# Dividing self-attention probabilities by their sums before they are turned, instead of dividing the attention output

## The reference

```python
qkv = jnp.roll(h @ w_qkv + b_qkv, -SHIFT, axis=1).reshape(B, nw, WIN, 3, H, D)
q, k, v = (qkv[:, :, :, 0], qkv[:, :, :, 1], qkv[:, :, :, 2])
scores = jnp.einsum('bnqhd,bnkhd->bnhqk', q, k) / jnp.sqrt(jnp.float32(D))
attn = jax.nn.softmax(scores, axis=-1)
o = jnp.einsum('bnhqk,bnkhd->bnqhd', attn, v).reshape(B, L, C)
x = x + (jnp.roll(o, SHIFT, axis=1) @ w_so + b_so) * g_msa
```

## Time and profile before

| what | value |
|---|---|
| median of 3 timed runs | 1449.89 us (1449.7 to 1450.29) |
| the profiled execution | 1451.27 us, with a span of 1449.4 us |
| mean granted TensorE clock | 0.989 of full speed |
| TensorE busy | 1414.2 us, 98% |
| VectorE busy | 1015.7 us, 70% |
| ScalarE busy | 838.8 us, 58% |
| GpSimd busy | 427.6 us, 30% |

### The profile page before, as it was taken

One profiled execution on the slowest core, in us unless ns is written; L12 is line 12 of the kernel. 1 busy time (PEld: TensorE's weight loads), 2 busy tenths in 40 slices (PEclk: granted clock), 3 DMA queues, 4 the chain that ended last, 5 costly groups with the idle time before them and its releaser, 6 DMA issues.

```text
span 1449.4 us, 30030 instructions
## 1 busy us (share of the span) xinstructions
PE 1414.2 (98%) x9753; PEld 1197.5 (83%) x9753; DVE 1015.7 (70%) x4628; ACT 838.8 (58%) x2555; POOL 427.6 (30%) x613
## 2 busy tenths in 40 slices
PE   7989999999999999999999999999999999999997
PEld 5778788888888888888888788888888888887886
DVE  3486859587695868769595786959586785958532
ACT  3474475757566385756647476664757457574433
POOL 1314132233324232331335132233334213232302
PEclk9889999999999999999999999999999999999999
DMA  7520000010000000010010000000010000000000
GB/s 244 190 78 2 1 4 23 2 33 9 19 30 16 1 2 25 1 34 5 22 32 1 15 2 15 11 24 11 9 48 1 16 1 8 2 1 9 1 4 12
DMA packets 27340, 34.98 MB, mean 24 GB/s; under 512 B 3324, under 2 KB 22448, under 8 KB 26929
## 3 DMA queue, kind: packets, MB, share of 16 engines
q1 hardware_dynamic: 27185, 33.07, 7.1%
HBM read 28.83 MB, written 4.22 MB: 23 GB/s over the span
## 4 chain that ended last, share of the span: by engine, by line
PE 88%; DVE 7%; ACT 2%; issue 1%; SPq 0%; POOL 0%; DMA 0%; DVEq 0%; ACTq 0%; POOLq 0%
PE bank L955 13%; PE bank L910 13%; PE bank L979 11%; PE bank L962 7%; PE bank L919 6%; PE bank L783 6%; PE bank L769 5%; PE bank L842 4%; PE bank L830 4%; PE bank L894 4%; PE bank L822 2%; DVE knocked L2172 2%; PE bank L754 2%; PE bank L740 2%; PE bank L804 1%
## 5 line engine op out<-in xcount | busy, mean ns | idle before, releaser
L910 PE MATMUL bank<-hB,Wm 128*128 128x256 f32 x1024 | 243.8, 384 | 2.2 <-ACT hB L1341 2.2
L910 PEld LDWEIGHTS bank<-hB,Wm 128*128 128x128 f32 x1024 | 191.6, 191 | 33.8 <-issue 7.0
L955 PE MATMUL bank<-nxT,W1nx 128*128 128x256 f32 x896 | 212.8, 384 | 0.0
L1380 ACT ACTIVATE prob<-bank,rmax 128x128 f32<-128x128 f32 x512 | 180.0, 434 | 27.6 <-DVE rmax L2120 27.6
L1731 POOL TENSOR_TENSOR scores<-scores,M 128x308 f32<-128x308 f32 x128 | 94.3, 737 | 320.0 <-DVE knocked L2172 317.5
L1387 ACT ACTIVATE probT<-bank 128x512 f32<-128x512 f32 (+1 forms) x256 | 139.7, 615 | 82.9 <-PE bank L894 76.7
L979 PE MATMUL bank<-W2p,gT 128*128 128x256 f32 x768 | 183.2, 381 | 3.0 <-DVE acc L2251 1.9
L955 PEld LDWEIGHTS bank<-nxT,W1nx 128*128 128x128 f32 x896 | 166.6, 191 | 23.4 <-issue 2.8
L979 PEld LDWEIGHTS bank<-W2p,gT 128*128 128x128 f32 x768 | 141.2, 190 | 23.8 <-issue 2.8
L1419 ACT ACTIVATE tbs<-bank,b1half 128x256 f32<-128x256 f32 x128 | 60.6, 473 | 144.9 <-PE bank L910 103.2
L1435 ACT ACTIVATE tbs<-bank,betaH 128x256 f32<-128x256 f32 x224 | 95.3, 487 | 83.1 <-PE bank L962 83.1
(11 more groups left out here) (230 smaller groups left out, 2710.1 us busy)
## 6 DMA issues: line engine op xcount, KB each, us to landing
Wm_g<-in_L_xcond_w_m_dram SPq DMA_DIRECT2D x4, 1024.0 KB, 5.5
W1ev<-in_L_xcond_e_w_dram SPq DMA_DIRECT2D x6, 512.0 KB, 7.4
x<-in_x_dram SPq DMA_DIRECT2D x16, 128.0 KB, 2.7
x<-in_x_dram SPq DMA_DIRECT2D x32, 64.0 KB, 2.3
Wm<-in_L_xcond_w_m_dram SPq DMA_DIRECT2D x1, 2048.0 KB, 9.0
out_dram<-acc SPq DMA_DIRECT2D x16, 128.0 KB, 1.7
out_dram<-acc SPq DMA_DIRECT2D x32, 64.0 KB, 2.0
batch_rows<-row_store SPq DMA_DIRECT2D x4, 384.0 KB, 3.7
```

The lines of the kernel that those rows point to most:

```text
L910: m = pe.matmul(bank_of(name)[:, half * UT:(half + 1) * UT], Wm1[:, k, c:c + P], hB[:, k, :], start=(k == 0), stop=(k == CB - 1))
L955: pe.matmul(bank_of(name)[:, n * UT:(n + 1) * UT], W1nx[:, k, c0 + n * P:c0 + (n + 1) * P], nxT[:, k, :], start=(n == 0 and k == 0), stop= ...
L1380: m = act.activation(prob[:, s, i, :], psum[s][:, i * P:(i + 1) * P], ACT.Exp, bias=rmax[:, t, s * HPS + i:s * HPS + i + 1], accum_out=rsu ...
```

## The change

Each slot's probabilities are divided before TensorE turns them. VectorE does this per slot in a new step `a_weigh`: a reciprocal of the slot's four sums and a multiply of the slot's 128x512 probabilities in place, after the slot's exponentials. TensorE's turning of a slot now waits for the semaphore `weighted` as well. In return the spreading, turning and copying of the inverses are gone for self-attention (cross-attention keeps its own), and the multiply at the end is a copy out of the bank. Sums are now stored in slot order.

```diff
 def a_turn_probs(t, s, u):
     wait_drained(pe, f"s{t}{s}", u)
+    pe.wait_ge(weighted, u * (TILES * SLOTS) + (t * SLOTS + s + 1))
...
-def a_invert_sums(u):
-    wait_drained(dve, f"s1{SLOTS - 1}", u)
-    dve.reciprocal(rinv[:, :, :], rsum[:, :, :]).then_inc(sums_inverted, 1)
+def a_weigh(t, s, u):
+    wait_drained(dve, f"s{t}{s}", u)
+    dve.reciprocal(rinv[:, t, s * HPS:(s + 1) * HPS], rsum[:, t, s * HPS:(s + 1) * HPS]).then_inc(sums_inverted, 1)
+    dve.wait_ge(sums_inverted, u * (TILES * SLOTS) + (t * SLOTS + s + 1))
+    dve.tensor_tensor(prob[:, s], prob[:, s], rinv[:, t, s * HPS:(s + 1) * HPS].rearrange("p (i a) -> p i a", a=1)
+                      .to_broadcast([P, HPS, P]), ALU.mult).then_inc(weighted, 1)
+def a_values_out(dst, u):
+    wait_full(dve, "pv", u)
+    dve.tensor_copy(dst.rearrange("p f t -> p (f t)"), bank_of("pv")[:, :]).then_inc(drained[JOB["pv"][0]], 1)
```

TensorE loses `a_turn_inverses("r1", "pv", ...)`, ScalarE `a_copy_inverses("r1", "pv", ...)` and GpSimd `a_spread("pv", ...)`, in the two prologue units and in `both`. VectorE's order in `both` becomes:

```diff
     a_max(0, (2,), a)
     a_max(0, (3,), a)
+    a_weigh(0, 0, a)
     b_route_norm(b)
+    a_weigh(0, 1, a)
     a_residual(xc, xc, "co", c)
+    a_weigh(0, 2, a)
     b_silu("h10", hE[:, 1], 0, b)
+    a_weigh(0, 3, a)
     wait_drained(dve, "co", c)
     ln_stats(2, xc, c)
     b_mix(0, b)
...
     a_max(1, (3,), a)
     b_silu("h11", hE[:, 1], 2, b)
-    a_invert_sums(a)
+    a_weigh(1, 0, a)
+    a_weigh(1, 1, a)
+    a_weigh(1, 2, a)
+    a_weigh(1, 3, a)
     ln_apply(2, xc, xnB, c)
-    a_normalise("pv", oT, a)
+    a_values_out(oT, a)
```

In the prologue VectorE weighs unit 0's slots (0,0), (0,1), (0,2) and (0,3) between the reads of the folded rows (`bv`, `g25`, `g8`), and (1,0) to (1,3) after the maxes of t = 1. In unit 1 the weighs stand between the top-k steps and picks of unit 0's cross-attention. Slot (1,3)'s stands ahead of the reads `p21`, `p20` and `r0`:

```diff
     a_max(1, (3,), 1)
+    a_weigh(1, 0, 1)
     a_pick(1, 1, 0)
+    a_weigh(1, 1, 1)
     a_sum_kept(0, 0)
+    a_weigh(1, 2, 1)
+    a_weigh(1, 3, 1)
     read_fold("p21", ...)
     read_fold("p20", ...)
     ...
     read_done("r0", dve.tensor_tensor(rrow[:, :], fold_psum("r0")[0:NB, 0:E], rrow[:, :], ALU.add))
```

More of the change, by code:

```diff
@@ L60 @@
 STAGE_C = {"xv", "r2", "co", "ln3"} | {f"{x}{t}{s}" for x in "cy" for t in range(TILES) for s in range(SLOTS)}
-STAGE_A = {"ln1", "k", "q", "v", "pv", "r1", "so", "ln2", "q2"} | \
+STAGE_A = {"ln1", "k", "q", "v", "pv", "so", "ln2", "q2"} | \
           {f"{x}{t}{s}" for x in "sp" for t in range(TILES) for s in range(SLOTS)}
@@ L298, in bass_pixart_experts @@
         row_max = sem("row_max")
-        sums_inverted, kept_inverted = sem("sums_inverted"), sem("kept_inverted")
+        weighted, sums_inverted, kept_inverted = sem("probabilities_weighted"), sem("sums_inverted"), sem("kept_inverted")
         spread_x = sem("kept_inverses_spread")
-        spread, kept_shifted, kept_exp, kept_sum = sem("inverses_spread"), sem("kept_shifted"), sem("kept_exp"), sem("kept_sum")
+        kept_shifted, kept_exp, kept_sum = sem("kept_shifted"), sem("kept_exp"), sem("kept_sum")
         topk, shifted, cross_exp, picked = sem("topk"), sem("shifted"), sem("cross_exp"), sem("picked")
@@ L851, in a_turn_inverses @@
             def a_turn_inverses(name, values, u):
-                pe.wait_ge(spread if values == "pv" else spread_x, u + 1)
+                pe.wait_ge(spread_x, u + 1)
                 wait_free(pe, name, u)
@@ L1029, in prologue @@
                 a_values(1, 0)
-                a_turn_inverses("r1", "pv", 0)
                 fold_anchor(1)
@@ L1073, in prologue @@
                 idle_products(5)
-                a_turn_inverses("r1", "pv", 1)
                 a_values(1, 1)
@@ L1202, in both @@
                 b_first_evidence("h21", 2 * RH + 2 * P, b)
-                a_turn_inverses("r1", "pv", a)
                 a_values(1, a)
@@ L1378, in a_exp @@
                 for i in range(HPS):
-                    h = head(s, i)
                     m = act.activation(prob[:, s, i, :], psum[s][:, i * P:(i + 1) * P], ACT.Exp,
-                                       bias=rmax[:, t, s * HPS + i:s * HPS + i + 1], accum_out=rsum[:, t, h:h + 1])
+                                       bias=rmax[:, t, s * HPS + i:s * HPS + i + 1], accum_out=rsum[:, t, s * HPS + i:s * HPS + i + 1])
                 m.then_inc(drained[s], 1)
@@ L1497, in prologue @@
                 a_copy_turned(1, 3, 0, "p")
-                a_copy_inverses("r1", "pv", 0)
                 act.wait_ge(doneA, 2)
@@ L1541, in prologue @@
                 a_kept_exp(1, 0)
-                a_copy_inverses("r1", "pv", 1)
                 a_copy_turned(0, 0, 0, "y", LC)
@@ L1622, in both @@
                 b_tanh_first("h20", hE[:, 0], 0, 8, b)
-                a_copy_inverses("r1", "pv", a)
                 b_tanh_first("h21", hE[:, 0], 2, 10, b)
@@ L1742, in a_spread @@
             def a_spread(values, u):
[L1744 to L1749, removed]
+                pool.wait_ge(kept_inverted, u + 1)
                 alone(pool)
                 for t in range(TILES):
-                    i = pool.tensor_copy(each[values][:, t], inv[:, t, :].rearrange("p (h a) -> p h a", a=1).to_broadcast([P, H, D]))
-                i.then_inc(spread if values == "pv" else spread_x, 1)
+                    i = pool.tensor_copy(each[values][:, t], kinv[:, t, :].rearrange("p (h a) -> p h a", a=1).to_broadcast([P, H, D]))
+                i.then_inc(spread_x, 1)
             def gate(w, n, b, done):
@@ L1836, in prologue @@
                 gate_co(0)
-                a_spread("pv", 0)
                 rstd_of(1, EPS0, 0)
@@ L1852, in prologue @@
                 a_shift_kept(1, 0)
-                a_spread("pv", 1)
                 a_spread("xv", 0)
@@ L1890, in both @@
                     gate_b(batch)
-                a_spread("pv", a)
                 rstd_of(2, EPS0, c)
@@ L2120, in a_max @@
                     dve.tensor_reduce(rmax[:, t, s * HPS:(s + 1) * HPS], slot_scores(s), AX.X, ALU.max, negate=True).then_inc(row_max, 1)
-            def a_invert_sums(u):
-                wait_drained(dve, f"s1{SLOTS - 1}", u)
-                dve.reciprocal(rinv[:, :, :], rsum[:, :, :]).then_inc(sums_inverted, 1)
+            def a_weigh(t, s, u):
[7 more added lines that the diff above has]
+                dve.tensor_copy(dst.rearrange("p f t -> p (f t)"), bank_of("pv")[:, :]).then_inc(drained[JOB["pv"][0]], 1)
             def a_normalise(name, dst, u):
                 wait_full(dve, name, u)
-                wait_drained(dve, "r1" if name == "pv" else "r2", u)
+                wait_drained(dve, "r2", u)
                 flat = lambda a: a.rearrange("p f t -> p (f t)")
@@ L2299, in prologue @@
                 dve.wait_ge(fold_full, FOLD_FULL["bv"])
+                a_weigh(0, 0, 0)
                 so_co = rows[:, 0:2, :].rearrange("b n c -> b (n c)")
@@ L2303, in prologue @@
                 dve.wait_ge(fold_full, FOLD_FULL["g25"])
+                a_weigh(0, 1, 0)
                 both_gates = gs[0:NB, :, :].rearrange("b s c -> b (s c)")
@@ L2308, in prologue @@
                 read_done("g8", dve.tensor_tensor(gate_rows[2], fold_psum("g8")[0:NB, 0:C], gate_rows[2], ALU.add))
+                a_weigh(0, 2, 0)
+                a_weigh(0, 3, 0)
                 gate_bias_rows()
@@ L2315, in prologue @@
                 a_max(1, (3,), 0)
-                a_invert_sums(0)
+                a_weigh(1, 0, 0)
+                a_weigh(1, 1, 0)
+                a_weigh(1, 2, 0)
+                a_weigh(1, 3, 0)
                 read_fold("p00", W2p[:, 0 * RB + 0:0 * RB + 2, :].rearrange("p k c -> p (k c)"), fold_psum("p00")[:, :])
                 read_fold("p01", W2p[:, 0 * RB + 2:0 * RB + 4, :].rearrange("p k c -> p (k c)"), fold_psum("p01")[:, :])
-                a_normalise("pv", oT, 0)
+                a_values_out(oT, 0)
                 a_residual(xs[0], xs[0], "so", 0)
@@ L2348, in prologue @@
                 a_topk("b", 1, 0, 0)
+                a_weigh(0, 0, 1)
                 a_pick(0, 1, 0)
+                a_weigh(0, 1, 1)
                 a_topk("a", 1, 2, 0)
+                a_weigh(0, 2, 1)
+                a_weigh(0, 3, 1)
                 a_topk("b", 1, 1, 0)
@@ L2369, in prologue @@
                 prepared_for_b()
-                a_invert_sums(1)
                 a_sum_kept(1, 0)
                 a_invert_kept(0)
-                a_normalise("pv", oT, 1)
+                a_values_out(oT, 1)
                 a_residual(xs[1], xs[1], "so", 1)
```

## The result

The changed kernel takes **1525.86 us** (median of 6 runs, 1524.28 to 1534.11) against 1450.09 for the kernel before (6 runs, 1449.49 to 1452.46): ratio 1.0521, with a 95% interval of 1.0508 to 1.0534. The forecast was 1530 us. The profiled execution took 1525.82 us against 1451.27, with a span of 1524.0 and a mean granted clock of 0.972; it is 74.6 us longer. The head of its page, beside the earlier trace rows: span, then busy time per engine.

A forecast was written before the change was run, and what follows sets the result against it. TensorE's instruction stream, busy 98% of the span, was taken as the bound. 14 x (3.30 - 0.53 + 2.3) = 71 plus 10 for the prologue made 81 us, 1532 profiled and 1530 forecast, range 1489 to 1553.

The forecast's parts named there:

- the clock: Behind each loop unit's stall: TensorE's idling lowers the granted clock to 0.50, costing 2.3 us per unit.
- the stall: Self-attention stage of each loop unit: TensorE waits for weighed slots (0,2) and (0,3), 0.6 then 2.7 us, 3.30 per unit.
- the transposes: Self-attention stage of each unit: four transposes of the inverses leave TensorE, saving 0.53 us per unit.
- the slots (1,s): Later slots of each loop unit: no added wait, taken at 0; up to 0.5 us where GpSimd gates a weight matrix.
- the prologue: Units 0 and 1, ahead of the loop: +2.6 and +5.4 us, with 2 for the clock, taken as 10.
- the read of `r0`: Prologue, unit 1: VectorE's read comes near 108.4 instead of 101.81, TensorE's router rows wait; +6.1 us, +5.4 after savings.
- the rule of halves: Wherever the granted clock is at 1.2 GHz: half of the low stretch is lost, 1.7 or 3.4 us.
- The clock holds: Rival for the loop: the stall comes but the clock does not drop; 1497 us, chance 0.18.
- No turns: Rival for slots (0,s): weighs and GpSimd's chain do not take turns, stall 0.72 us per unit; 1461 us, chance 0.12.
- Faster: Rival: every slot is ready before TensorE asks, leaving 8.5 us less of TensorE; 1441 us, chance 0.06.

The follow-up runs named there:

- e1: Changed kernel with the weigh's multiply reading the slot's scores from PSUM instead of its probabilities from SBUF, exponentials left out of the weights; 1466.20 us.
- e2: Changed kernel with GpSimd's mixed-bias operations cut to 2 columns per tile instead of 256; 1471.70 us.
- e5: Kernel before with the division left out: inverses, their spreading, turning and copying gone, values copied out, no weigh; 1444.16 us.
- e4b: Changed kernel with idle products filling TensorE's stall, 2 ahead of turning slot (0,2) and 11 ahead of (0,3); 1505.59 us.
- e8: Changed kernel with VectorE's read of `r0` moved ahead of the weigh of slot (1,0) in unit 1 of the prologue; 1521.80 us.
- e6: Changed kernel with the weighed probabilities written to a spare tile and TensorE turning the undivided ones without waiting for `weighted`; 1465.03 us.
- e3: Changed kernel with the router's normalisation moved in the loop from behind weigh (0,0) to behind weigh (0,3) on VectorE; 1480.33 us.
- e9: Kernel before with per-slot division in the loop only, router normalisation after weigh (0,3), GpSimd's chain split, more TensorE work ahead of slot (0,3); 1446.93 us.
- e4: Changed kernel with idle products on TensorE, 4 ahead of turning slot (0,2) and 22 ahead of (0,3); 1539.91 us.

## Why the prediction was right

It named the stage, the slots and the mechanism, and its own time line for them holds to a tenth of a microsecond. Its sum is less good than the 4 us between 1530 and 1525.86 look. For the profiled execution it added up 81 us, and 74.6 was measured. One term, the clock, was 10 us too high; the stall, the transposes, the slots (1,s) and the prologue were each 1 to 1.5 us too low, 5 together. That they took back half of the one large error is luck.

**The weighs and the stall (forecast 3.30 per unit, measured 3.38).** The forecast put the ends of the weighs (0,0) to (0,3) at T-0.44, +1.70, +3.15 and +6.28; they are at T-0.44, +1.70, +3.15 and +6.28. TensorE was to start (0,2) and (0,3) at T+3.21 and +6.34 and does at T+3.30 and +6.42, 0.08 later: the forecast took 0.06 us from VectorE's end to TensorE's start, and behind these waits it is 0.15 (640.79 to 640.94). That a broadcast second input counts as an SBUF input was the one link without a row; e1 and e2 show it from both sides.

The Trainium skill ("SBUF — State Buffer", section "SBUF: two separate sides") calls the shared ports an exclusive lock for the whole instruction. The runs agree but for 0.14 us: VectorE's 0.69 us operation ends 0.55 us behind the end of GpSimd's in three places. Every one of e1's multiplies, with one SBUF input, takes 0.69.

**The transposes removed (0.53 per unit).** e5 measures 0.42 per unit: 5.9 us in 14 units instead of 7.4. A group of four in the middle of this stream is worth a little less than its start-to-start time; why isn't shown.

**The slots (1,s) (taken at 0).** Right for 11 units. In the three with a weight matrix (1,3) waits 0.16 and is some 0.3 late, about 1 us in all; the forecast's bound was 0.5 each.

**The clock (forecast 2.3 per unit, 1.3 to 1.6 found).** This is the term that was mis-sized. The forecast took a short low stretch and a bit in every unit. The changed kernel has one in 11 of 14, nine of 3.41 us and two of 6.83, so by halves 22.2 us, 1.6 per unit, instead of 32.2. e4b shows that it is the idling: with the same delay and TensorE kept at work it is gone. It also gives the measured price, 17.2 us in 13 units, 1.3 per unit. Which units are spared (5, 12 and 13 here, 5 and 13 in e8) no row before the change could tell.

**The prologue (forecast 10, measured 11.4).** Right in size, with its parts misplaced. Unit 0 was to give 2.6 and gave 5.5: five of its slots wait, 4.7 us together, against one of 0.74 before. Unit 1 was to give 5.4 and 2 of clock and gave 5.9. Its reasoning put all on the read of `r0`, which e8 shows to be worth 3.0 with its clock. It had four weighs queue behind slot (1,3)'s last exponential and the fifth end 4.1 us after it; in the changed kernel (1,3)'s alone stands behind it and ends 0.9 after (110.22 against 109.28), since VectorE weighs the others while ScalarE is still at work. What else unit 1 lost goes with two things: the waits for the weighs themselves, 6.4 us in six places against 2.2 in four for the exponentials before, and the clock, low for 17.1 us between 90 and 120 us against 6.8 before. How the other 3 us divide between them isn't shown. The longest waits, 2.74 and 1.63, stand at (0,s), which the forecast had not listed for this unit.

**Together.** Stall 47.3, transposes -5.9, clock 22.2, gating units 1, prologue 11.4 make 76, and 74.6 was measured. The difference is mostly the rule of halves: with e4b's 17.2 us in place of the 18.8 of its 13 units the sum is 74.4. A unit was to take 5 us longer and takes 4.4 on average (57.7 in 13).

**The rivals.** "The clock holds" (1497) is what e4b builds, at 1506. "No turns" (1461) is what e1 builds, at 1466. "Faster" (1441) named the right threshold, the weigh of (0,3) before T+3.0, and its gain is about e5's (6.8 of 8.5); but e6 shows that it left out a price. The forecast took 6.5 us of VectorE per unit as costless wherever nothing waits for the weigh, and the late mix of expert 0 says it isn't: 0.85 us per unit.

## What to carry to other kernels

Before an operation with two SBUF inputs is added to VectorE, write GpSimd's and VectorE's two-input operations of that stage on one time axis with TensorE's requests: where they met here they ran one after the other, and the sum of the lengths decided, not the busy shares. Moving one of them only moves the meeting point, so the whole unit must be written out (e3 against e9); where the large input can be read from PSUM the meeting is gone (e1). And a step that takes work off the bounding engine is worth what it takes off only if the new wait ends before the engine asks, and if the work it adds elsewhere holds up nothing else (e6); here a stall of 3.4 us cost another 1.3 through the clock.

## What the runs showed of the hardware that was not expected

- One float32 product of 128 columns out of 128x128 weights costs TensorE 0.23 us and leaves two records (e4, 22 products: 44 records, 5.08 us). Who sizes a filler from records must halve the count.
- Beside a steady row of GpSimd multiplies of 128x256, VectorE's weigh takes 1.01 to 1.02 us every time (12 of 12 in the changed kernel, and 12 of 12 in e9), not 0.69 and not 1.5, and most of GpSimd's take 1.17 us instead of 0.73; beside multiplies of 128x512 the weigh takes up to 1.55.
- A stall in two pieces, 0.53 and 2.5 us with four transposes between, is followed by 3.4 or 6.8 us at 1.2 GHz in 11 of 14 units; pieces of 0.60 or 0.66 alone (e1, e2) never are in the loop.
- The clock in the prologue differs between profiled executions of kernels that are alike up to there: 6.8 us at 1.2 GHz from 28 us on in e1 and e2, 3.4 from 29 us in e3 and e4, none there in the changed kernel. In e1 and e2 T of unit 0 is 3.5 us later.
